# A decoder's last expert stage: rows routed and sent out group by group inside the attention before it

## The reference

```python
x = x + mamba(layernorm(x))                      # state space scan
x = x + relu_attention(layernorm(x), context)
x = x + attention_and_experts0(layernorm(x))     # 8 experts and a shared one
x = x + recurrence(layernorm(x))                 # h = tanh(x_t + h Wh)
x = x + dual_attention(layernorm(x), context)    # softmax over x and over the context, 16 heads
x = x + experts1(layernorm(x))
```

```python
gate_scores = sigmoid(xf @ gate_w.T + balance_bias)         # (4096, 8)
topk_scores, topk_idx = top_k(gate_scores, 2)
topk_scores = topk_scores / (topk_scores.sum(-1, keepdims=True) + 1e-6)
comb = zeros((T, 8)).at[arange(T)[:, None], topk_idx].add(topk_scores)
h = silu(einsum('td,ehd->teh', xf, w1))                     # 256 -> 512
expert_out = einsum('teh,edh->ted', h, w2)                  # 512 -> 256
out = einsum('te,ted->td', comb, expert_out)
```

## Time and profile before

| | us |
|---|---|
| median of three runs | 3620.92 |
| profiled execution, own time | 3619.14 |
| its span, first to last instruction | 3617.3 |
| PE busy | 2767.1 (76%) |
| DVE busy | 2010.7 (56%) |
| POOL busy | 1405.4 (39%) |
| granted clock of TensorE, mean | 0.892 of full speed |

### The profile page before, as it was taken

The page is one execution under the profiler, slowest core; times in us unless marked ns, Lnnn a source line. Parts: engine busy times, 40 slices in busy tenths (PEclk is TensorE's granted clock), DMA queues, the critical chain, the costliest instruction groups (busy, mean ns, idle before and its releaser), DMA issues. The chain is left out here.

```text
span 3617.3 us, 50700 instructions
## 1 busy us (share of the span) xinstructions
PE 2767.1 (76%) x16564; PEld 1869.4 (52%) x16564; DVE 2010.7 (56%) x3307; ACT 1483.1 (41%) x2600; POOL 1405.4 (39%) x1516
## 2 busy tenths in 40 slices
PE   4777777766775888787999996995888986329990
PEld 1232223224554555545888863993555564128880
DVE  3888888875886678741222235104888887401113
ACT  3555555534664556421222212223766664302320
POOL 2566666653444566533000043001554444350006
PEclk8887887888998999988999998997999998669995
DMA  2000000000022000023666631001000000136654
GB/s 73 0 1 1 1 0 0 0 0 27 18 67 71 1 1 1 1 78 125 197 194 193 194 113 41 1 1 31 7 13 7 7 7 2 36 126 212 211 186 139
DMA packets 107038, 215.82 MB, mean 60 GB/s; under 512 B 13200, under 2 KB 71824, under 8 KB 101392
## 3 DMA queue, kind: packets, MB, share of 16 engines
q1 hardware_dynamic: 94576, 180.03, 15.9%
q0 software_dynamic: 12288, 33.57, 2.9%
HBM read 161.92 MB, written 51.64 MB: 59 GB/s over the span
## 5 line engine op out<-in xcount | busy, mean ns | idle before, releaser
L498 POOL TENSOR_TENSOR u_in<-dtx,b_rep 128x512 f32<-128x512 f32 x256 | 333.9, 1324 | 237.9 <-ACT b_rep L479 228.3
L471 PE MATMUL PS<-scaled,ident 128*128 128x512 f32 x512 | 325.3, 722 | 75.7 <-DVE scaled L508 75.6
L514 DVE TENSOR_TENSOR_SCAN state<-PS,u_in 128x512 f32<-128x512 f32 x256 | 311.3, 1219 | 76.9 <-POOL u_in L498 34.3
L1815 PE MATMUL PS<-d_unit_T,d_w 128*128 128x256 f32 x1248 | 284.0, 381 | 1.0 <-ACT d_unit_T L1825 1.0
L487 ACT ACTIVATE PS<-dt,decay_rate 128x508 f32<-128x508 f32 x256 | 174.2, 685 | 262.4 <-DVE state L514 262.3
L1093 POOL TENSOR_TENSOR e_hs<-e_pr 128x512 f32<-128x512 f32 x128 | 164.1, 1282 | 283.1 <-ACT e_pr L1060 283.1
L1836 ACT ACTIVATE d_act_b<-PS 128x256 f32<-128x256 f32 (+1 forms) x188 | 78.9, 420 | 472.8 <-PE PS L1815 472.8
L1848 DVE TENSOR_TENSOR d_hid<-d_act_b,PS 128x256 f32<-128x256 f32 (+1 forms) x188 | 87.6, 466 | 315.6 <-ACT d_act_b L1836 315.6
L1815 PEld LDWEIGHTS PS<-d_unit_T,d_w 128*128 128x128 f32 x1248 | 235.2, 191 | 32.0 <-issue 1.4
L996 DVE TENSOR_REDUCE e_mx<-PS 128x8 f32<-128x1024 f32 x128 | 156.2, 1220 | 95.2 <-PE PS L939 95.1
L1773 PE MATMUL PS<-d_w,d_hid 128*128 128x256 f32 x880 | 199.4, 381 | 2.1 <-DVE d_hid L1848 2.1
(11 more groups left out here) (416 smaller groups left out, 6345.3 us busy)
## 6 DMA issues: line engine op xcount, KB each, us to landing
d_w<-in_d_w SPq DMA_DIRECT2D x41, 1024.0 KB, 5.0
f_w<-in_f_w SPq DMA_DIRECT2D x78, 512.0 KB, 4.2
d_w<-in_d_w SPq DMA_DIRECT2D x41, 512.0 KB, 4.0
rows_by_expert<-zeros SPq DMA_DIRECT2D x39, 256.0 KB, 2.4
d_unit_rows<-rows_by_expert SPq DMA_DIRECT2D x39, 256.0 KB, 3.9
out_by_expert<-d_y_rows SPq DMA_DIRECT2D x39, 256.0 KB, 4.0
f_unit_rows<-rows_by_expert SPq DMA_DIRECT2D x39, 256.0 KB, 3.9
out_by_expert<-f_y_rows SPq DMA_DIRECT2D x39, 256.0 KB, 4.1
```

The lines of the kernel that those rows point to most:

```text
L471: nc.tensor.matmul(YB[:, c], ident[:], scaled[:, (KD * n + c) % RC], start=False, stop=n == NS - 1).then_inc(m_y, 1)
L498: nc.gpsimd.tensor_tensor(u_in[:, k % RU], dtx[:, p, c], b_rep[:, n % RB], ALU.mult).then_inc(m_u, 1)
L514: nc.vector.tensor_tensor_scan(state[:, k % 2], DECAY[:, k % RD], u_in[:, k % RU], 0.0, ALU.mult, ALU.add).then_inc(m_h, 1)
L1815: step = nc.tensor.matmul(b, wt[:, r, c, f * 128:f * 128 + 128], x, start=c == 0, stop=c == KD - 1)
```

## The change

Layernorm, logits, top 2 and the sending of rows for experts f are moved into attention e. A new set of side generators (`early_router`, with due steps `ROUTE`) handles group g - 1 in turn g, after its output projection; the last group's stands behind the last turn. The turns of attention e stand in straight code now, and `PLAN["e"]` has other due steps. Each expert has a fixed region of 4096 rows in `rows_in_place`, so a slot needs only the count so far (`run`), which PE adds to the rank within the group, and not the totals of all groups. A row is 272 elements: 256 features, the 8 weights and the number of its token. The regions are filled with blank rows (weights 0, a token number out of bounds) during mamba, 136 transfers of 256 rows. The table of units is made after the last group's count. SyncE stores each group of X to the output during attention. In the new stage `list_experts` a unit's result is multiplied by its weight as it leaves PSUM and added onto the output in DRAM by two indirect transfers with an add, token numbers out of bounds being left out; the store to a list, the 64 gathers and the adds into X fall away. Rows and weights come in a ring of 3, weights in one transfer of 1 MB.

```diff
+    E, REGION = 8, NG * GT
+    ROW = D + 2 * E
+    rows_in_place = nc.dram_tensor("rows_in_place", (E * REGION + E * UR, ROW), F32, kind="Internal").ap()
+    emptied, blank_set, in_place = sem("emptied"), sem("blank_set"), [sem("in_place0"), sem("in_place1")]
...
+    BLANKS = (E * REGION + E * UR) // UR
+    blank = mamba_mem.take("blank", [128, UR // 128, ROW])
...
+        nc.gpsimd.memset(blank[:, :, 0:D + E], 0.0)
+        nc.gpsimd.memset(blank[:, :, D + E:ROW], float(2 * NG * GT)).then_inc(blank_set, 1)
...
+    def early_router(tag, mem, table, FB, number, full, empty, x_in, plan):
...
+        def setup_vector(dve):
+            nc.vector.memset(ones[:], 1.0)
+            for e in range(E):
+                nc.vector.memset(run[:, e:e + 1], float(e * REGION // 128))
+            nc.vector.memset(rows[:], 0.0).then_inc(made, 1)
...
+        def rows_vector(dve, g, p):
+            yield plan["stats"]
+            dve.wait_ge(x_in, 2 * g + 2)
+            after(dve, counted, g)
+            for k in range(GS):
+                step = nc.vector.bn_stats(st[:, k], X[:, g, k])
+            step.then_inc(counted, 1)
+            dve.wait_ge(counted, g + 1)
+            after(dve, scaled, g)
+            for k in range(GS):
+                step = nc.vector.bn_aggr(mvs[:, k], st[:, k])
+            step.then_inc(mean, 1)
+            yield plan["add"]
+            dve.wait_ge(full, number("rows", g, KD) + 1)
+            nc.vector.tensor_tensor(lg[:], sums, v["v"][:].unsqueeze(1).broadcast_to([128, GS, E]), ALU.add).then_inc(empty, 1)
...
+        def rows_scalar(act, g, p):
+            yield plan["norm"]
+            act.wait_ge(scaled, g + 1)
+            after(act, in_list[p], 16 * SCATTERS * (g // 2))
+            after(act, full, number("rows", g - 2, 1) + 1 if g > 1 else 0)
+            for k in range(GS):
+                step = nc.scalar.activation(rows[:, p, k, 0:D], X[:, g, k], ACT.Identity, bias=rs[:, 3, k:k + 1],
+                                            scale=rs[:, 1, k:k + 1])
+            step.then_inc(normed, 1)
+            for c in range(KD):
+                yield plan["taken"][c]
+                act.wait_ge(full, number("rows", g, c) + 1)
+                nc.scalar.activation(xT[:, c], FB, ACT.Copy).then_inc(empty, 1)
...
+        def rows_tensor(pe, g, p):
+            for c in range(KD):
+                yield plan["turn"][c]
+                after(pe, empty, number("rows", g, c))
+                pe.wait_ge(normed, g + 1)
+                for k in range(GS):
+                    step = nc.tensor.transpose(FB[:, k * L:k * L + L], rows[:, p, k, c * 128:c * 128 + 128], ident[:])
+                step.then_inc(full, 1)
+            yield plan["turn"][KD]
+            pe.wait_ge(empty, number("rows", g, KD))
+            for k in range(GS):
+                for c in range(KD):
+                    step = nc.tensor.matmul(FB[:, k * E:k * E + E], xT[:, c, k * L:k * L + L], wr_k[:, c], start=c == 0, stop=c == KD - 1)
+            step.then_inc(full, 1)
...
+        def rank_tensor(pe, g, p):
+            yield plan["rank"]
+            pe.wait_ge(empty, number("rank", g, 0))
+            pe.wait_ge(chose, g + 1)
+            picks = chosen.rearrange("p k e -> p (k e)")
+            nc.tensor.matmul(FB[:, 0:GS * E], before_me, picks, start=True, stop=False)
+            for d in range(1, GS):
+                nc.tensor.matmul(FB[:, d * E:GS * E], ones[:], picks[:, 0:(GS - d) * E], start=False, stop=False)
+            nc.tensor.matmul(FB[:, 0:GS * E], ones[:], run[:].unsqueeze(1).broadcast_to([128, GS, E]), start=False, stop=True).then_inc(full, 1)
...
+            yield plan["route"][0]
+            dve.wait_ge(exped, g + 1)
+            link(V.tensor_scalar(lg[:], lg[:], 1.0, None, ALU.add))
+            link(V.reciprocal(lg[:], lg[:]))
+            for j in range(TOP):
+                if j:
+                    yield plan["route"][1]
+                link(V.tensor_reduce(top[:, j], lg[:], AX.X, ALU.max))
+                link(V.tensor_tensor(tmp[:], lg[:], over_e(top[:, j]), ALU.is_equal))
+                link(V.tensor_tensor(tmp[:], tmp[:], order.unsqueeze(1).broadcast_to([128, GS, E]), ALU.mult))
+                link(V.tensor_reduce(part[:], tmp[:], AX.X, ALU.max))
+                link(V.tensor_tensor(best[:, j], tmp[:], over_e(part[:]), ALU.is_equal))
+                if j == 0:
+                    link(V.scalar_tensor_tensor(out=lg[:], in0=best[:, 0], scalar=-2.0, in1=lg[:], op0=ALU.mult, op1=ALU.add))
+            V.tensor_tensor(chosen[:], best[:, 0], best[:, 1], ALU.add).then_inc(chose, 1)
+            yield plan["route"][2]
+            link(V.tensor_tensor(part[:], top[:, 0], top[:, 1], ALU.add))
+            link(V.tensor_scalar(part[:], part[:], 1e-6, None, ALU.add))
+            link(V.reciprocal(part[:], part[:]))
+            link(V.tensor_tensor(weight[:], top[:], part[:].unsqueeze(1).broadcast_to([128, TOP, GS]), ALU.mult))
+            link(V.tensor_tensor(both[:], best[:], weight[:].unsqueeze(3).broadcast_to([128, TOP, GS, E]), ALU.mult))
+            after(dve, in_list[p], 16 * SCATTERS * (g // 2))
+            link(V.tensor_tensor(rows[:, p, :, D:D + E], both[:, 0], both[:, 1], ALU.add))
+            link(V.tensor_copy(rows[:, p, :, D + E], tokens[:, g * GS:g * GS + GS]))
+            dve.wait_ge(chose, g + 1)
+            link(V.tensor_reduce(so_far[:], chosen.rearrange("p k e -> p e k"), AX.X, ALU.add))
+            yield plan["route"][3]
+            dve.wait_ge(full, number("rank", g, 0) + 1)
+            V.tensor_tensor(both[:], best[:], sums.unsqueeze(1).broadcast_to([128, TOP, GS, E]), ALU.mult).then_inc(empty, 1)
+            dve.wait_ge(empty, number("rank", g, 0) + 1)
+            link(V.tensor_tensor(run[:], run[:], so_far[:], ALU.add))
+            link(V.tensor_reduce(slot_f[:], both.rearrange("p j k e -> p (j k) e"), AX.X, ALU.add))
+            V.tensor_copy(slot[:, p], slot_f[:]).then_inc(placed, 1)
+            link.turn_over()
...
+        def rank_pool(pool, g, p):
+            for k in range(GS):
+                for j in range(TOP):
+                    yield plan["scatter"][2 * k + j]
+                    if k == j == 0:
+                        if g == 0:
+                            pool.wait_ge(emptied, 16 * BLANKS)
+                        pool.wait_ge(normed, g + 1)
+                        pool.wait_ge(placed, g + 1)
+                    nc.gpsimd.indirect_dma_start(rows_in_place, bass.IndirectOffsetOnAxis(slot[:, p, j * GS + k:j * GS + k + 1], 0),
+                                                 rows[:, p, k], None).then_inc(in_list[p], 16)
...
-        "e": dict(front=[2, 2, 8, 12, 18, 22, 28, 32, 52, 58, 62, 68], taken=[2, 4, 8, 14, 18, 24, 28, 34, 54, 58, 64, 68],
-                  back=[38, 42], out_at=[38, 48], early=[36, 40, 42]),
+        "e": dict(front=[10, 12, 15, 18, 22, 38, 40, 55, 58, 62, 68, 72], taken=[12, 14, 8, 18, 24, 36, 38, 54, 58, 64, 66, 78],
+                  back=[2, 8], out_at=[4, 6], early=[36, 40, 44]),
     }
-
-    def attention(tag, turn, sets, relu=False, rms=None, out_w=None):
+    ROUTE = dict(stats=12, scale=14, norm=22, turn=[28, 30, 32], taken=[28, 28], add=34,
+                 exp=36, route=[42, 44, 46, 52], rank=48,
+                 scatter=[50, 60, 60, 64, 64, 70, 78, 78])
...
+                if table and g > 0:
+                    sides.append(router["rows"][n](eng, g - 1, 1 - p))
+                if table and g > 0:
+                    sides.append(router["rank"][n](eng, g - 1, 1 - p))
...
+                for g in range(NG):
+                    turn(g, g % 2)
+                alone(back(eng, NG - 1, 1))
+                alone(router["rows"][n](eng, NG - 1, 1))
+                alone(router["rank"][n](eng, NG - 1, 1))
...
+                    for g in range(2, NG + 2):
+                        if g < NG:
+                            load_ctx(sp, g, g % 2)
+                        store_x(sp, g - 2)
...
+        def sync(sp):
+            for u in range(UNITS):
+                r = u % RING
+                after(sp, turned, u - RING + 1)
+                after(sp, sent_to, u - RING + 1)
+                at = sp.value_load(table["start_i"][:].unsqueeze(2)[0:1, u], min_val=0, max_val=E * REGION // UR + E - 1)
+                sp.dma_start(rows[:, r], unit_of[:, at]).then_inc(row_in[r], 16)
+                e = sp.value_load(table["expert_i"][:].unsqueeze(2)[0:1, u], min_val=0, max_val=E - 1)
+                after(sp, down, UT * (u - RING + 1))
+                sp.dma_start(w[:, r], ins[f"{tag}_w"][e]).then_inc(w_in[r], 16)
+            sp.wait_ge(stored, 16 * NG)
...
+        def output_tensor(pe, u):
+            pe.wait_ge(hidden, FC * u + FC)
+            for r in range(UT):
+                after(pe, mixed, UT * (u - 1) + r + 1)
+                for f in range(FC):
```

(54 more changed lines are left out.)

194 lines of the change are left out of this document (187 added, 7 removed).

## The result

The changed kernel takes 3500.11 us (median of 4 runs, 3496.35 to 3503.35) against 3619.40 (3611.32 to 3625.28): a ratio of 0.967, interval 0.965 to 0.969. Faster, as forecast, and inside the stated range of 3405 to 3530, but 55 us above the 3445 of the likeliest case and outside that case's own range (3420 to 3480). The profiled span is 3494.6 us, 52.9 over the 3441.7 of the sum.

The account below looks back on a forecast made before the run. PE and DVE near their limit in attention, PE in the unit loop, POOL's indirect transfers in two idle parts; 3617.3 - 127 - 88.6 + 34 + 6 = 3441.7 us of span, forecast median 3445, range 3405 to 3530.

Parts of the forecast that it names:

- the likeliest case: Whole kernel: the summed forecast of 3445 us as a median, own range 3420 to 3480, chance 0.60.
- Parts 1, 2 and 5: In order: head before first expert product falls from 169.9 to 43 us; tail falls to 6; attention setups add 6.
- part 3: Unit loop: 289.5 us bound by PE stay; the adding scatters, a cycle of 5.7 us within 7.37 a unit, cost 0.
- L: Unit loop: landing time of an adding scatter, taken as 4.1 us; no cost as long as it is under 5.8.
- Part 4: Attention turns: routing and new steps add 4.7 us in each of six turns and 6 in the last, 34 in all.
- 3.8 of waits: Attention turns: the trace's 69.0 us less the pair sum of 65.2, kept unchanged for the new plan.
- One or two scatters at a time: nothing: Attention turns: scatters issued singly or in twos (2.5 us) fit POOL's idle between sums and cost nothing.
- the slack takes 2: Last attention turn, without projections: DVE gets 8 us of router work, slack absorbs 2, so 6 are added.
- Rival A: Attention: the router does not fit; up to the bound of 87 us, 53 more, 3498 in total; chance 0.18.
- B: Unit loop: the adds bound it; with a landing of 7.5 us, 66 more, 3511 in total; chance 0.14.
- C: Attention: the router is hidden whole, 34 us less, 3411 in total; chance 0.04.
- D: Unit loop: unoverlapped landings of the adds make the kernel slower than before; 3688 us at a 12 us landing; chance 0.04.

## Why the prediction was right and where it was wrong

Parts 1, 2 and 5 held, and part 3 in its result. Head 46.3 against 43 (logits 1.2 and barrier 2.3 too low, in bounds); tail 10.3 against 6 (0.8 us from the last y to the first issue, two issues of 1.55 us and not 0.96, 5.6 for the landing and the end); unit loop unchanged, with the landing of 4.7 near the 4.1 taken. Setup and first turn +4.9 against +6. In the unit loop the sum behind the "nothing" was off: a cycle of 0.3 + 1.27 + L = 5.7, with room for L up to 5.8. Measured are 0.9 + 1.86 + L against 7.4, so L had room up to 4.7, which is its measured median. That this part cost nothing was partly luck. The blank transfers (landing 5.3 us each) hid in the first stage and were through at 137 us: the second stage's loads were issued at 809.5, before the change at 815.1.

Of the rule weighed in part 3 (the Trainium skill, DMA: Bandwidth & Descriptors, Latency and other measured facts): an added 2 us at high load, the estimate from that page, would have been L = 6.1 and a cycle over 7.37. The runs show 4.7, nearer the row than the page's estimate, and 6.1 only under doubled adds.

Part 4 failed: 11.7 us a turn for 4.7, and 33.1 for 14.4 at the end. Its step was to take the larger sum of PE and DVE in each pair, each instruction at its undisturbed price, and to keep 3.8 of waits. By the table the 7.0 that are missing, net of the waits kept, are pair 5 (2.6), pair 4 (1.9), pair 2 (1.3), pair 0 (1.1) and little else.
- Pairs 4 and 0: DVE is the bound as predicted, but at 14.1 and 11.1, not 11.8 and 9.5. What was missing is the price of meeting POOL. In pair 4 the copies beside POOL's sums (1.25 and 1.11 us instead of 0.17 and 0.36) are 1.8 of it. In pair 0 the add to X and `e_oT` (1.77 and 0.92 us instead of 0.69 and 0.29) are 1.7. The prediction weighed such meetings only for POOL's scatters and let POOL's idle time take them; it was DVE that paid.
- Pair 2: 8.1, not 6.8. The sum had no ACT in it, and ACT is busy 7.7 of the 8.1.
- Pair 5: no engine's sum is large. At full clock it takes 9.3, so some 1.8 of its 11.1 is the granted clock, for which the sum had no term. Without routing it takes 12.5, some 1.5 of it with the clock; moving PE's and ACT's side products to other steps brings it to 8.7, so the rest is their order. The sum of an engine can't show that.
- Pair 1: 10.2 for 10.3, but PE, named as its bound, is busy 7.9 of it. That number was luck.
- Pair 7: 8.9, and 8.8 before, against my 6.7 in both plans. The likeness is luck. In the kernel before the pair takes 7.5 us in the one turn at full clock and 8.0 to 10.4 where the clock is at 0.79 to 0.91. In the changed kernel the clock is full, and `e_rec` takes 1.50 us instead of 0.36 beside POOL's sum.
- "One or two scatters at a time: nothing": they cost 0.7 us a turn in pair 0 and up to 2.3 in all.
- The last turn: "the slack takes 2", for a price of 6. Its pairs 0 to 5 took 49.3 us before, 53.3 with the new steps alone and 60.7 with routing: 11.4 more, 7.4 of it the routing. Without projections DVE isn't freer in pair 4, which is again 14.1 us long (3105.6 to 3119.7).

Rival A named the time, 3498, and its sign showed: turns over 77 us. Its bound was 87 us for attention after the setup, and 87.4 were measured. The agreement is luck: the 87.4 are 42.4 for the routing and 55.2 for the new steps, less 10.2 for straight code, while A had seven turns of 12.4 for the routing alone. Its reason holds by half: the routing doesn't fit in the slack, but the steps moved for it cost more than it did. B, C and D are excluded by PE's 0.5 us of idle in the loop and by the turns.

What stays open: what pair 1 waits for, what decides how long the clock stays down in a turn, how much of the stretched DVE work outside pairs 0 and 4 costs time, and whether steps exist that hold the routing for under 80 us a turn. The routing on the old steps wasn't tried: the group's output comes out at 38 and 42 there, behind the steps at which the routing needs it.

## What to carry to other kernels

When work is woven into a loop whose engines run in fixed orders, price it by the order: for each added or moved product ask what stands behind it on its engine and who frees its buffer. The larger engine's sum, ACT and POOL included, is only a lower bound. Ask too which of DVE's instructions will run beside POOL's after the move: here such instructions were 5.7 us a turn over their shortest times. Where the trace of before lies above the sum in one pair (8.8 against 6.7 here), look at the granted clock of that pair and at its waits before carrying the difference over. Price the moved neighbours with the new work, since either alone misleads.

## What the runs showed of the hardware

An adding indirect transfer of 128 rows of 256 elements costs GpSimd 1555 ns an issue, a plain one of 272 elements 960 to 1030, and lands in 4.7 us beside 203 GB/s of other traffic, a plain one in 2.4 to 2.5. Doubling the adds took the scratch ones' landing to 6.1.

A DVE copy of 128 x 4 elements took 0.17 us behind the last turn and 1.25 within a turn, where it ended with a POOL `tensor_tensor` of 1.26 us. The Trainium skill (SBUF — State Buffer, Who interferes with whom) tells of an exclusive lock between DVE's two-port modes and GpSimd; the trace agrees, and here the smallest copy paid nearly the whole of GpSimd's instruction. A DVE add of 128 x 512 elements, both inputs in SBUF, took 0.69 us alone and 1.77 beside two such POOL instructions.

One turn of the same kernel took 78.9 us at a mean granted clock of 0.98 and the next 81.4 at 0.92, with PE busy 64.2 and 68.0 us for the same work. While the clock was at its lower level (1.2 GHz), 32 products of 128 columns took 1.93 us for 1.08.
